# Modulation, weight pieces and loads as steps of their own in a planned four-layer transformer kernel

## The reference

```python
mod = silu(c) @ w_mod + b_mod                 # one row per batch: 6 x 144 numbers
sh1, sc1, g1, sh2, sc2, g2 = split(mod, 6)
qkv = (ln(x) * (1 + sc1) + sh1) @ w_qkv + b   # 144 -> 432, 16 heads of 9
# layer 0 only: q = ln(q)*g_q, k = ln(k)*g_k, over the 9 numbers of a head
x = x + g1 * (softmax(q @ k.T / 3) @ v @ w_proj + b)
x = x + g2 * mlp(ln(x) * (1 + sc2) + sh2)     # 144 -> 576 -> 144, gelu
# layer 1: x += (x U R - x U) U.T ; U from a QR of P, R = expm(skew(silu(c) @ W.T + b))
# layer 2: like layer 0, without the norms of q and k
# layer 3: like layer 2, but four expert MLPs, weighted by the top two of a gate
```

## Time and profile before

| | us |
|---|---|
| three runs | 1468.55, 1470.41, 1455.7 |
| median | 1468.55 |
| the profiled execution, its own time | 1463.1 |
| its span | 1461.3 |
| what lies around the span | 1.8 |
| TensorE busy in the span | 1326.6 |
| VectorE, ScalarE, POOL busy | 957.0, 920.3, 585.2 |

### The profile page before, as it was taken

The page is one execution under the profiler, slowest core; times in us unless marked ns, Lnnn a source line. Parts: engine busy times, 40 slices in busy tenths (PEclk is TensorE's granted clock), DMA queues, the critical chain, the costliest instruction groups (busy, mean ns, idle before and its releaser), DMA issues. The chain is left out here.

```text
span 1461.3 us, 35869 instructions
## 1 busy us (share of the span) xinstructions
PE 1326.6 (91%) x13200; PEld 1065.8 (73%) x13200; DVE 957.0 (65%) x2818; ACT 920.3 (63%) x1808; POOL 585.2 (40%) x670
## 2 busy tenths in 40 slices
PE   6687899888898999988889999999999999999998
PEld 2346577666776777557677777778888888888887
DVE  4367888888787745687777868775656565554331
ACT  2264667667677645657766777676666667766642
POOL 3354779879778623122333333332121211211110
PEclk9587899999999997998899999999999999999999
DMA  5221111111111110124222222121111111112100
GB/s 148 57 79 46 35 50 35 51 40 41 44 48 43 53 41 19 45 63 126 67 65 61 69 61 72 55 72 33 43 46 45 40 47 32 48 30 56 43 8 21
DMA packets 97924, 75.90 MB, mean 52 GB/s; under 512 B 25520, under 2 KB 83163, under 8 KB 97622
## 3 DMA queue, kind: packets, MB, share of 16 engines
q1 hardware_dynamic: 97750, 73.60, 18.1%
HBM read 43.04 MB, written 28.95 MB: 49 GB/s over the span
## 5 line engine op out<-in xcount | busy, mean ns | idle before, releaser
L1682 PE MATMUL p_B<-s_pC,s_H 128*128 128x144 f32 (+1 forms) x1920 | 253.6, 288 | 0.4 <-ACT s_JS L1105 0.3
L1682 PEld LDWEIGHTS p_B<-s_pC,s_H 128*128 128x128 f32 (+1 forms) x1920 | 242.8, 191 | 3.7 <-ACT s_JS L1105 0.5
L1303 DVE TENSOR_REDUCE s_MX<-p_S 128x16 f32<-128x2048 f32 x96 | 219.1, 2282 | 23.2 <-PE p_S L1611 22.6
L1029 ACT ACTIVATE s_Pm<-p_S 128x2048 f32<-128x2048 f32 x96 | 180.3, 1878 | 46.9 <-PE p_S L1625 46.1
L894 POOL TENSOR_TENSOR s_s<-s_s,s_half 128x32 f32<-128x32 f32 x32 | 175.9, 5499 | 38.4 <-DVE s_s L1271 38.3
L1075 ACT ACTIVATE s_H<-p_B,s_pC 128x512 f32<-128x512 f32 (+1 forms) x218 | 143.9, 686 | 52.1 <-PE p_B L1547 51.0
L890 POOL TENSOR_TENSOR s_OC<-s_OC,s_RB 72x256 f32<-72x256 f32 x96 | 71.6, 747 | 256.0 <-DMA s_RB<-sums 255.8
L1553 PE MATMUL p_B<-s_eye,s_QK 128*128 128x128 f32 x764 | 120.3, 290 | 7.8 <-DVE s_HS L1525 2.2
L898 POOL TENSOR_TENSOR s_X<-s_X,s_GA 128x144 f32<-128x144 f32 x96 | 49.0, 510 | 187.7 <-DVE s_GA L1322 187.6
L1553 PEld LDWEIGHTS p_B<-s_eye,s_QK 128*128 128x128 f32 x764 | 90.0, 147 | 27.2 <-issue 9.6
L863 POOL TENSOR_SCALAR s_XHA<-s_X,s_MVA,s_VEA 128x48 f32<-128x48 f32 x96 | 52.9, 563 | 119.5 <-PE p_B L1585 118.9
(11 more groups left out here) (303 smaller groups left out, 3109.3 us busy)
## 6 DMA issues: line engine op xcount, KB each, us to landing
heads<-s_OT SPq DMA_DIRECT2D x96, 256.0 KB, 2.2
s_GA<-gates SPq DMA_DIRECT2D x96, 72.0 KB, 3.0
s_GM<-gates SPq DMA_DIRECT2D x48, 144.0 KB, 3.3
s_OC<-heads SPq DMA_DIRECT2D x192, 36.0 KB
s_RB<-sums SPq DMA_DIRECT2D x192, 36.0 KB
s_QT<-s_MS SPq DMA_DIRECT2D x192, 8.0 KB
s_SG<-in_main SPq DMA_DIRECT2D x33, 72.0 KB, 2.1
out<-s_X SPq DMA_DIRECT2D x8, 288.0 KB, 2.6
```

What stands on the lines that cost most here:

```text
L1029: e.activation(Pm[n % 2][:, :], bank["s2", i][:, :], ACT.Exp, scale=SCALE).then_inc(SEM["ex"], 1)
L1303: e.tensor_reduce(MX[n % 2][:, :], bank["s1", i][:, :].rearrange("p (h k) -> p h k", h=NH), AX.X, ALU.max, negate=True).then_inc(SEM["mx"], 1)
L1682: ins = e.matmul(bk[:, 256 * i2:256 * i2 + C], H[k % 2][0:n, c, 128 * t:128 * t + 128], w2[l][0:n, 5 * x + c, :], start=(c == 0), stop=(c ...
```

## The change

`mod` becomes seven kinds of step: `mw` (SP loads the weights of layers 2 and 3), `ma` (one pair of matmuls, twice), `mc` (the copy of one pair), `ms` (the spread), `mo` (the transposes), `mv` (the copies out) and `mg` (SP writes the gates to DRAM). `wt` becomes `wd` (SP's load), `wc` (the mean off, pieces 0 and 1 only), `wt` (the rounding on ScalarE) and `wl` (the rest on VectorE); `pk` loads the packed weights of a part, `xl` the parts of `x`, `el` the small tables. Each has a position of its own, and only `rt` is still held to a common order. The staging buffer gets a third slot (`NSG`). In the dry run a DMA now has a size: the queue works through them at 170 bytes per ns, one after another, and then 2.0 us pass instead of 2.2. All tables of positions have new numbers. Every instruction of the computation is still there; with the new positions and waits the number of fillers goes from 263 to 339.

```diff
-NGA = 3
+NGA, NSG = 3, 3
-MIXED = ("mod", "wt", "rt")
+MIXED = ("rt",)
-LAND, LOAD, TURN = 2200, 1300, 60
+LAND, LOAD, TURN = 2000, 1300, 60
+RATE = 170
...
         else:
             s, k = doing[e]
+            if e == "sp":
+                queue = max(queue, now) + parts[e][s][k].size / RATE
             for x in parts[e][s][k].signals:
-                events.append((now + (LAND if parts[e][s][k].table == "dma" else HOP[e]), count, e, x))
+                events.append(((queue + LAND if e == "sp" else now + HOP[e]), count, e, x))
...
-TILE = {"qkv": (-0.94, -1.036, -0.428), "v": (-1.428, -0.529, -0.266), "n1": (-0.816, 0.921, 1.004), "n2": (0.02, 1.154, 1.392),
+TILE = {"qkv": (-0.963, -0.805, -0.291), "v": (-1.16, -1.224, -0.166), "n1": (-0.807, 0.422, 2.831), "n2": (0.04, 0.646, 2.34),
...
+    for l in LAY:
+        s = START[f"mod {l}"]
+        put(s - 1.5, "mw", l)
+        for hf in range(2):
+            put(s + 0.1 * hf, "ma", l, hf)
+            put(s + 0.1 * hf + 0.05, "mc", l, hf)
+        for k, stage in enumerate(("ms", "mo", "mv")):
+            put(s + 0.2 + 0.05 * k, stage, l)
+        put(s + START["gates"], "mg", l)
+
+    def pieces(l, part, s, step):
+        first = min(j for j, p in enumerate(PIECES) if p[0] == l and p[1] == part)
+        put(s - 0.3, "pk", l, part)
+        for j in range(first, last_piece(l, part) + 1):
+            put(s + step * (j - first) - START["piece"], "wd", j)
+            for k, stage in enumerate(("wc", "wt", "wl")):
+                if stage != "wc" or j < 2:
+                    put(s + step * (j - first) + 0.05 * k, stage, j)
...
-        SG, SGS = sb("SG", [128, 2, SGC]), sb("SGS", [80, 2, SGC])
+        SG, SGS = sb("SG", [128, NSG, SGC]), sb("SGS", [80, NSG, SGC])
...
+                elif stage == "wd":
+                    j = i[0]
+                    l, part, c0, c = PIECES[j]
+                    k = j % NSG
+                    if j >= NSG:
+                        w.wait_ge(*at("wl", j - NSG))
```

More of the change, by code:

```diff
@@ L85, in __init__ @@
     def __init__(self, waits, ns, table):
-        self.waits, self.ns, self.table, self.signals = waits, ns, table, []
+        self.waits, self.ns, self.table, self.signals, self.size = waits, ns, table, [], 0
     def then_inc(self, sem, by):
@@ L232, in plan @@
     work, slow, window = deque(), 2, WINDOW
-    gap = None
+    gap, queue = None, 0.0
     def met(waits):
@@ L267, in begin @@
         kind = bank_kind(s[0]) if e == "pe" else None
[L268 to L269 removed]
+        if kind:
             if kind == "S":
[L271 removed]
+                bank[s] = tuple(idle["S"])
                 idle["S"].clear()
             else:
[L274 to L276 removed]
+                bank[s] = (idle["B"] or idle["S"]).popleft(),
+            before[s] = {last[b] for b in bank[s] if b in last}
+            held.setdefault(s if s[0] in IN_PLACE else freed_by(*s), []).append(s)
         return True
@@ L386, in n_pos @@
         return n + (0.0, START["layer 2"], START["layer 3"])[n // B]
-    put(-9.0, "mod", 0)
-    for j in range(last_piece(0, "q") + 1):
-        put(-8.5 + 0.1 * j, "wt", j)
-    for j in range(last_piece(0, "q") + 1, last_piece(0, "f") + 1):
-        put(0.5 + 0.3 * (j - 3), "wt", j)
-    put(2.0, "mod", 2)
-    put(3.0, "mod", 3)
-    for j in range(last_piece(0, "f") + 1, last_piece(2, "q") + 1):
-        put(6.0 + 0.3 * (j - 8), "wt", j)
+    for l in LAY:
[15 more added lines that the diff above has]
+                    put(s + step * (j - first) + 0.05 * k, stage, j)
+    pieces(0, "q", START["wq 0"], 0.1)
+    pieces(0, "f", START["wf 0"], START["wf step"])
+    pieces(2, "q", START["wq 2"], 0.3)
+    for k in range(1, 4):
+        put(START["x"] + START["x step"] * k, "xl", k)
+    put(START["x"] + 2 * START["x step"], "el")
     for u in range(NA // 2):
@@ L448, in order @@
             if m == NG - 1:
-                for j in range(last_piece(2, "q") + 1, last_piece(2, "f") + 1):
-                    put(p + 2.4 + 0.2 * (j - 11), "wt", j)
-                for j in range(last_piece(2, "f") + 1, len(PIECES)):
-                    put(s + 1.5 + 0.3 * (j - 16), "wt", j)
+                pieces(2, "f", p + START["wf 2"], 0.2)
+                pieces(3, "q", s + START["wq 3"], 0.3)
+                pieces(3, "f", s + START["wq 3"] + 0.9, 0.3)
     for k in range(D):
```

200 lines of the change are left out of this document (101 added, 99 removed), and 14 rows, old and new, of the table TILE.

## The result

The changed kernel takes 1413.89 us (median; 1408.37 to 1418.53), the kernel before 1466.06 us beside it. The ratio is 0.9653, 95% interval [0.9589, 0.9716]: 3.5% faster, some 52 us. The forecast was 1447 with a range from 1425 to 1481, so the sign was right and the size about a third of what came. The profiled executions took 1463.1 and 1408.37 us, their spans 1461.3 and 1406.6 us: 54.7 us between them. The changed kernel's profile is that of its fastest run.

What follows compares the result with a forecast made beforehand. It saw waiting at the start, list order deciding in most of layer 0, and TensorE's own work in layer 3. Terms -15.5 - 7 + 7 - 1 = -16.5 from 1463.1 gave 1447 us, range 1425 to 1481.

Steps and rivals of the forecast that it cites:

- the 15.5 us are what the stall itself is worth: At the start: TensorE's waits of 12.2 us at layer 2's modulation transposes and 3.3 for its weights go, -15.5 us.
- 7 us for the clock: From 37 to 73 us: TensorE's work runs at a higher clock than 0.59, -7 us, bounds 0 and -8.6.
- The two smaller handovers: At the modulation's transposes: TensorE's remaining waits for ScalarE's copies, 2.3 us, expected to stay.
- The walk: Following the new list through the start to the first qkv: 26 to 34 us, taken as 30 instead of 57.
- The fillers at +7: 76 more fillers, 61 behind the first qkv: half their 14.5 us full cost was booked, +7 us.
- The third slot at -1: Layer 3's weight pieces: saves part of ScalarE's one 3.8 us load wait, -1 us, bounds 0 and -3.8.
- All the other numbers: Layers 2 and 3: new positions shift the order by a few places, taken as 0 us.
- the bound of 9 us: Layers 2 and 3: most a new order may win or lose, half of TensorE's 18.5 us lacking from 700 to 900.
- The sum's high side, 1459: Whole kernel: start as walked (-22.5), fillers in full (+14.5) and a wait at the loads (+3.8).
- The low side, 1426: Whole kernel: -15.5, -8.6, -3.8 and -9 from 1463.1, with fillers at nothing.
- the start is taken back in layer 0: Rival: QR steps or POOL's powers set layer 0's end, so the early start only adds waiting; 1463 to 1470, chance 0.27.
- The slow rival: Layers 0 and 2: fillers ahead of ready work and new order cost more than the start gives; 1478 to 1484, chance 0.13.

Runs made afterwards that it cites:

- e8: Changed kernel, lists untouched, with 120 more fillers ahead of the first qkv as a pure delay; 1445.09 us, 0.986 of the kernel before.
- h1: Changed kernel's code with written order: the changed kernel's up to about the first projection, the kernel before's behind it; 1463.49 us, ratio 0.9996.
- h6: Control: changed kernel's code, third slot included, with the order of the kernel before throughout and 492 fillers; 1474.89 us, ratio 1.0071.
- e5: Kernel before, with each filler between the first rotation step and layer 2's first qkv issued three times; 1472.42 us, ratio 1.0048.
- n1: Changed kernel with its dry run's load landing time at 2030 ns instead of 2000; ratio 0.9919 to the kernel before.
- n4: Kernel before with 61 ns instead of 60 added to a TensorE step in its dry run; ratio 1.0144.
- h4: Changed kernel's code with written order: the changed kernel's up to the exp of tile 4, the kernel before's from there; 1444.5 us, ratio 0.986.
- e1: Changed kernel's code with all numbers of the kernel before (tables, positions, two slots, old landing time); 1494.43 us, ratio 1.0181.
- e2: Changed kernel with the general tables of the kernel before, all else of the change kept; 1468.55 us, ratio 0.9972.
- n2: Changed kernel with 61 ns instead of 60 added to a TensorE step in its dry run; ratio 0.9994 to the kernel before.
- n3: Kernel before with its dry run's load landing time at 2230 ns instead of 2200; ratio 1.0339.
- e7: Changed kernel with loads waiting for the reader two pieces back, seen by the dry run, which made other lists; 1466.52 us, ratio 0.9997.
- e3: Kernel before with only its general tables replaced by the changed kernel's; 1507.71 us, ratio 1.0264.

## Why the prediction was right or wrong

**Where it looked was right.** The first `qkv` at 28.1 is inside 26 to 34, the wait of the transposes is gone, the clock from 37 to 73 us is 0.81 where above 0.8 was asked for, the first projection is 39 us earlier where 30 was said, and layers 2 and 3 (0.1 and -6.3 us) are within the 9 us. The fillers take 101 us where 95 to 100 was said, and TensorE's idle time is down by more than that. One sign was missed: the first `qkv` of layer 2 comes at 520.9, where 550 was said.

**The step that failed most: "the 15.5 us are what the stall itself is worth".** I had walked to a first `qkv` 27 us earlier and then booked the wait that went, with 7 us for the clock, 22.5 in all. Measured at the first exp it is 34.5, and e8 shows that such a lead is handed on in full in this order. The reason that I gave for the smaller number, that two steps of `e1` and a modulation now come behind `qkv`, was a good worry: in h1 the steps pushed back do eat the lead. In the changed order they lie beside the attention without making it longer: the lead is 34.5 at tile 0 and 38.0 at tile 4. The two smaller handovers of 2.3 us, which were to stay, went as well. The walk was the better measure; the wait was only its largest single piece, and the waits for loads and for clock behind it went too.

**The fillers at +7.** The sign is wrong. I priced them as steps in front of ready work; without any the kernel loses 40 us. I had given the clock a term at the start only; in layer 0 TensorE's own work is 12.4 us shorter, at a clock of 0.96 instead of 0.90. What the 76 added ones give was not measured by itself: they come with the new order. The control h6 (229 more, +10 us with all else that it has) and e5 (58 more, 0.5% or 7 us) show that fillers added to an order without need cost a little on balance, about 0.05 us (10/229) and 0.12 us (7/58) each. In e5 that balance is 9.8 us of fillers against 9.1 us won by the clock.

**The third slot at -1.** It is 9 us by the ratios, whose intervals overlap, 17 by the medians and 20 by the profile, in lists that count on it. I read one wait of 3.8 us for a load in layer 3 and said that layer 0's share was in the walk to the first `qkv`. That walk isn't touched by it (27.8); the loads queued at SP behind the waiting piece are what is late at the first exp, and I had named them only for a later tile.

**No term for the order of layer 0.** "All the other numbers" was a term for layers 2 and 3 alone. Layer 0 with the way to layer 2 gave another 14.0 us in the profile, of which e5 and e8 put the 6.9 on the way down to the clock there. And the bound of 9 us for what a new order can do was far too narrow: n1 to n4 move layers 2 and 3 by 26 to 46 us with a change that means nothing. The sum's high side, 1459, left even that bound out, and took the clock's 7 us as sure: with both it would have been 1475. The low side, 1426, had every term at its best and is still 12 us above what was measured.

**The rivals.** That the start is taken back in layer 0 is just what happens in h1, h4, e1, e2 and the neighbours n1 and n2, so 0.27 was not too much for it. But it isn't the QR or POOL's powers that take it back: in the changed order, by e8, neither sets the pace, and in h1 it is the wait for the last `e1`'s way through DRAM. It is the order of the lists. The Trainium skill's advice ("Perfetto Trace Analysis", section "Identifying the Most-Contended Engine") to begin with the busiest engine stood with this rival. The measurement decides against the strict reading: the largest piece came out of the stretch in which TensorE was least busy (67.5 of 98.3 us), and TensorE's own work took less time (1244.4 to 1204.5 us) though none of it was taken away. The slow rival, fillers and new order that cost more than the start gives, is what e1 and n3 show of other lists.

**What of the 52 us belongs to the change and what to the fit.** Like must be compared with like: fitted with fitted gives 0.965; neighbour with neighbour gives 0.9919/1.0339 = 0.959 for one number and 0.9994/1.0144 = 0.985 for the other, and crosswise 0.978 and 0.967. All kernels with the changed code whose lists the dry run chose anew (e1, e2, e7, n1, n2) lie between 0.992 and 1.018, those with the code of before (e3, n3, n4) between 1.014 and 1.034. So the change is worth something in both pairs, 22 to 60 us, and an early start is the part that all the kernels of the first kind have. But against the kernel before, whose list is fitted, it can't be seen without a list made for it: with one that isn't, the same change reads as -0.8 to +1.8%. Two pairs are few, and how much of the 14 us in layer 0 is the new description (the queue's rate, the positions of loads) and how much a lucky list stays open. That this part of it is luck alone is not excluded by any run.

## What to carry to other kernels

Value a shorter start by walking to the first step of the steady loop in the new list, and take that difference, not the wait that goes; it is a measure only as long as the steps behind are ready too (in n3 a first `qkv` 26 us early gave 15 at the first exp). Then ask where the steps that were pushed back will lie, and which of them wait for a way through DRAM. Where a dry run sets the order, a change of structure and its tuned numbers can't be judged apart: each alone read as nothing or a loss. Before crediting a mechanism, move a meaningless number a little in both kernels; if that costs more than the effect, compare neighbour with neighbour.

## What the hardware showed that I had not expected

- TensorE's work without fillers takes 1204.5 us at a mean granted clock of 0.971 and 1293.3 us at 0.903, with the same lists. 101 us of work that computes nothing save 40 us of the kernel's time.
- The clock can also be bought at its own price: on the way to layer 2, 58 more fillers raised it from 0.79 to 1.00, the own work got 9.1 us shorter, and the fillers took 9.8 us.
- Small waits and a lower clock came together. The neighbour n1 has the same start; in layer 0 its clock is 0.91 instead of 0.96, it has 11.7 us more of idle time, and TensorE's own work takes 20 us more (399.3, 379.1).
- With two slots SP waits for readers of pieces for 33.5 us up to 75 us, 21.6 more than with three. At the first exp that made only 7 us, most of it in waits of TensorE for what stood behind the pieces in SP's list or hung on it.
